# Layer norm's scaling moved from VectorE to ScalarE in a two-layer adaLN transformer kernel

## The chip, the cores and the metric

One core of a Trainium2 chip runs one launch of the kernel. The metric is the device time of a launch in microseconds. Instruction times are those of one profiled execution.

## The reference, cut to what matters

Two batches of 2048 tokens of width 128 pass through two layers. Every layer normalises its input, modulates it (a scale and a shift per feature that depend on the batch), runs attention, and does the same again ahead of a feed-forward part. Layer 0 has rotary attention and an FP4 feed-forward net, layer 1 causal attention and a mixture of experts.

```python
def _layernorm(x, axis=-1, eps=1e-05):
    m = jnp.mean(x, axis=axis, keepdims=True)
    v = jnp.var(x, axis=axis, keepdims=True)
    return (x - m) / jnp.sqrt(v + eps)

# layer 0
h = _layernorm(x) * (1 + ca) + sa
x = x + ga * _L0_attn_ref(h, Wq, Wk, Wv)        # softmax over 2048 keys, mask tril(k=1)
h = _layernorm(x) * (1 + cb) + sb
x = x + gb * _L0_ffn_ref(h, ...)                # x and h quantised to FP4 in blocks of 16
# layer 1
h = _layernorm(x) * (1 + ca) + sa
x = x + ga * _L1_attn_ref(h, qk, ov)            # causal
h = _layernorm(x) * (1 + cb) + sb
x = x + gb * _L1_ffn_ref(h, ...)                # router, 8 experts and a shared one
```

## The kernel before, in words

A batch is 16 tiles of 128 tokens, in 4 groups of 4 tiles. The program runs both batches one after the other through a loop of 32 **slots**: slot s holds layer s // 16, query tile s % 16. Every engine has its own program, written out by hand in the order of the slots, and waits for the others by semaphores. Nothing reorders the work: what stands behind a waiting instruction on its engine waits too.

In slot s, TensorE (`pe`) first transposes the normalised groups that are due (`input_turns`, `turn_group`), computes the first chunk of the next tile's scores (`scores(s + 1, 0)`, into PSUM bank 0), and then goes over the chunks of up to 512 keys: `turn_probs` transposes the probabilities of chunk c, `gate_up`, `turn_hq` and `down` are the FP4 net of an earlier tile, `scores(s + 1, c + 1)` follows, and `values` multiplies the previous chunk with V. All transposes go through one PSUM bank (`TURN`), so each waits until ScalarE has copied the one before it out. `scores(s + 2, 0)`, at the start of slot s + 1, waits until ScalarE has taken the exponential of chunk 0 of tile s + 1, since it overwrites that bank.

ScalarE (`act`) starts slot s with the exponentials of chunks 0 and 1 (`exp`), copies the transposed groups (`copy_group`), and then in each chunk copies the transposed probabilities (`copy_probs`), takes `tanh` for the FP4 net, copies `hq`, and takes the exponential of chunk c + 2. VectorE (`dve`) takes the row maxima, multiplies the rotary tables, quantises to FP4 (`quantise_h`, `fp4_input`), and ends slot s with `finish`: divide by the row sum, add to x, and take the statistics (`bn_stats`) of the finished tile. When a group's fourth tile is done, `bn_aggr` gives mean and variance (`send_statistics`), GpSimd (`pool`) raises the variance to the power -0.5 (L473), and VectorE normalises: four instructions of 128x128, `(x - mean) * rstd` (`normalise`, L1320; for the first two groups of a batch `first_normalise`, L1227).

Four norms per group are told apart. **norm0** feeds layer 0's attention (groups 2 and 3 normalised in slots 1 and 3; groups 0 and 1 of the next batch in slots 27 and 29, or in the setup). **norm1** feeds the FP4 net: normalised in slots 4, 8, 12, 16, modulated by GpSimd (`modulate_1`, L493 and L495), quantised by VectorE at the slot's end (`fp4_input`), scaled by GpSimd (`xq_scaled`), transposed by TensorE two slots later (L696 in the trace). **norm2** feeds layer 1's attention: normalised in slots 12, 16, 20, 24, transposed at the start of the next slot (L595 in the trace), copied by ScalarE twice (L1027, L1029). **norm3** feeds the router: slots 21, 25, 29, and one after the last slot.

The order on VectorE in a slot, before: `normalise_in_slot` stands behind the maxima and ahead of `quantise_h` and `finish`.

```python
for c in range(1, following):
    maximum(s + 1, c)
normalise_in_slot(s)
...
if ffn_tile(s, FFN_LAG) is not None:
    quantise_h(s - FFN_LAG)
...
finish(s)
if group_at(s, FP4_SLOT) is not None:
    fp4_input(group_at(s, FP4_SLOT))
```

## Time and profile before

| | |
|---|---|
| median of 3 runs | 736.52 us (735.71 to 736.78) |
| the profiled execution | 740.21 us, span of its instructions 738.4 us |
| TensorE busy | 647.3 us, 88% of the span |
| VectorE busy | 511.4 us, 69% |
| ScalarE busy | 319.5 us, 43% |
| GpSimd busy | 222.5 us, 30% |
| slots of batch 0, of batch 1 | from 37.9 to 329.4 us, from 329.4 to about 619 us |

Both batches go through the same program, and the trace shows the same times in the second, some 290 us later; so rows are given for batch 0. The setup comes ahead of them, and the mixture of experts behind them. A row of the timeline gives the start, the duration, the engine and the line of one or several instructions; in square brackets stands how long the engine was idle before it, and what released it. PE is TensorE, DVE VectorE, ACT ScalarE, POOL GpSimd.

### The profile page before, as it was taken

To read this page: it belongs to the slowest core of one execution; us is meant where nothing else is said; L and a number is where in the kernel's file an instruction comes from. 1 tells how busy PE (TensorE), PEld (TensorE's weight loads), DVE (VectorE), ACT (ScalarE), POOL (GpSimd) and SP (SyncE) were. 2 spreads that over 40 slices of the span, in tenths; PEclk is the share of its full clock that TensorE was granted. 3 is DMA by queue.
4 is the path that set the end of the run, shared out by engine and by line. 5 is a ranking of instruction groups with operands and counts; after the bars stand their busy time and mean duration, and the time that the engine had idled before them with its cause. 6 is when DMAs were issued, how large, how long until landed. Compare 5 with 4: busy or idle time off the path is not lost.

```text
span 738.4 us, 11039 instructions
## 1 busy us (share of the span) xinstructions
PE 647.3 (88%) x3816; PEld 504.9 (68%) x3828; DVE 511.4 (69%) x1465; ACT 319.5 (43%) x644; POOL 222.5 (30%) x225
## 2 busy tenths in 40 slices
PE   5889799988777999988889989958889998799997
PEld 4456687877556778775678777846677786576674
DVE  5957598696768667726669777596865754876665
ACT  1133344445234454543344444523445453554453
POOL 3333654343545211004455435253421102000000
PEclk9989999999879999999999999978999999999999
DMA  8400000000000000000000000000000000000001
GB/s 262 110 0 1 2 1 1 1 0 1 1 0 1 1 1 1 1 1 1 1 1 1 1 1 2 1 1 0 1 1 1 1 1 1 0 16 29 14 19 40
DMA packets 12078, 9.64 MB, mean 13 GB/s; under 512 B 1708, under 2 KB 10744, under 8 KB 12024
## 3 DMA queue, kind: packets, MB, share of 16 engines
q1 hardware_dynamic: 12024, 8.94, 4.1%
q8 instruction: 31, 0.51, 0.3%
q14 instruction: 23, 0.19, 0.1%
HBM read 6.84 MB, written 2.10 MB: 12 GB/s over the span
## 4 chain that ended last, share of the span: by engine, by line
PE 69%; DVE 18%; ACT 5%; POOL 4%; issue 4%; DMA 1%; SPq 0%; ACTq 0%; POOLq 0%
PE ps L777 14%; PE ps L647 12%; PE ps L755 8%; PE ps L606 5%; DVE xn L1320 5%; PE ps L922 4%; PE ps L924 4%; PE ps L923 4%; PE ps L800 3%; PE ps L665 2%; PE ps L801 2%; PE ps L595 2%; PE ps L816 2%; DVE row_max L1357 1%; PE ps L601 1%
## 5 line engine op out<-in xcount | busy, mean ns | idle before, releaser
L1083 ACT ACTIVATE probsT<-ps 128x512 f32<-128x512 f32 (+3 forms) x160 | 85.2, 533 | 180.4 <-PE ps L755 180.4
L777 PE MATMUL ps<-v_sb,probsT 128*128 128x129 f32 (+1 forms) x1148 | 157.1, 280 | 3.7 <-ACT probsT L1085 3.7
L777 PEld LDWEIGHTS ps<-v_sb,probsT 128*128 128x128 f32 (+1 forms) x1148 | 141.5, 191 | 10.6 <-ACT probsT L1085 5.5
L1357 DVE TENSOR_REDUCE row_max<-ps 128x1 f32<-128x512 f32 (+2 forms) x144 | 87.6, 619 | 48.3 <-PE ps L647 18.1
L755 PE MATMUL ps<-ident,probs 128*128 128x128 f32 (+1 forms) x574 | 95.7, 285 | 16.7 <-ACT probsT L1083 6.0
L755 PEld LDWEIGHTS ps<-ident,probs 128*128 128x128 f32 (+1 forms) x574 | 67.5, 143 | 49.0 <-issue 45.3
L1057 ACT ACTIVATE probs<-ps,neg_max 128x512 f32<-128x512 f32 (+7 forms) x158 | 92.8, 618 | 16.9 <-DVE neg_max L1364 16.0
L473 POOL TENSOR_TENSOR rstd<-veps,half 128x4 f32<-128x4 f32 x34 | 34.2, 1012 | 154.1 <-DVE veps L1211 153.9
L501 POOL TENSOR_TENSOR hq<-ha,hp 128x352 f32<-128x352 f32 x32 | 29.9, 934 | 139.5 <-DVE hp L1398 139.5
L647 PE MATMUL ps<-k_high,q_high 128*128 128x512 f32 (+4 forms) x112 | 46.0, 411 | 0.6 <-ACT probs L1005 0.6
L1152 ACT ACTIVATE probs<-ps 128x512 f32<-128x512 f32 x40 | 24.0, 599 | 44.7 <-PE ps L924 44.7
L1320 DVE TENSOR_SCALAR xn<-x_sb,mv,rstd 128x128 f32<-128x128 f32 x112 | 41.4, 435 | 2.2 <-POOL rstd L473 2.2
L1590 DVE TENSOR_TENSOR probs<-probs,ps 128x512 f32<-128x512 f32 x40 | 27.5, 687 | 19.9 <-ACT probs L1152 19.4
L1412 DVE SCALAR_TENSOR_TENSOR silu_g<-silu_g,ps 128x352 f32<-128x352 f32 x32 | 16.5, 516 | 34.1 <-ACT silu_g L1065 34.1
L922 PE MATMUL ps<-q_high,h_high 128*128 128x512 f32 x80 | 38.8, 485 | 0.8 <-DVE q_high L1523 0.8
L1372 DVE RECIPROCAL rsum<-ps 128x1 f32<-128x1 f32 x64 | 10.4, 163 | 40.8 <-PE ps L777 40.5
L647 PE MATMUL ps<-k_high,q_low 128*128 128x512 f32 (+4 forms) x112 | 38.7, 345 | 0.0
L647 PE MATMUL ps<-k_low,q_high 128*128 128x512 f32 (+4 forms) x112 | 38.3, 342 | 0.0
L647 PE MATMUL ps<-h_high,q_high 128*128 128x512 f32 (+2 forms) x80 | 36.9, 461 | 0.5 <-ACT probs L1057 0.5
L595 PE MATMUL ps<-ident,xn 128*128 128x128 f32 x100 | 17.6, 304 | 18.9 <-DVE xn L1320 18.0
L800 PE MATMUL ps<-w_guT,xqT 128*128 128x352 f32 x64 | 29.8, 553 | 4.6 <-ACT v_sb L998 2.5
L924 PE MATMUL ps<-q_high,h_low 128*128 128x512 f32 x80 | 32.2, 403 | 0.0
(240 smaller groups left out, 1380.8 us busy)
## 6 DMA issues: line engine op xcount, KB each, us to landing
out<-x_sb SPq DMA_DIRECT2D x8, 256.0 KB, 2.3
x_sb<-in_L_attn_x SPq DMA_DIRECT2D x2, 512.0 KB, 5.3
hT_all<-in_L_wmod SPq DMA_DIRECT2D x2, 384.0 KB
rope_cos<-table_cos SPq DMA_DIRECT2D x1, 768.0 KB, 7.5
rope_sin<-table_sin SPq DMA_DIRECT2D x1, 768.0 KB, 9.1
rope_cos<-table_cos SPq DMA_DIRECT2D x1, 256.0 KB, 4.1
rope_sin<-table_sin SPq DMA_DIRECT2D x1, 256.0 KB, 5.1
moe_raw<-in_L_ffn_expert_gate_w SPq DMA_DIRECT2D x1, 256.0 KB, 4.2
```

The source lines that it names most:

```text
L473: pool.tensor_tensor(rstd[:, kind, :], veps[:, kind, :], half[:], ALU.pow).then_inc(rstd_ready[kind], 1)
L606: pe.matmul(bank(dst), w[:], hT[:, g * BANK:(g + 1) * BANK], start=True, stop=True).then_inc(proj_ready, 1)
L647: mm = pe.matmul(ps[:, cols], q_parts[q][:, tile], keys[k][:, cols], start=(n == 0), stop=(stop and n == len(passes) - 1))
L755: mm = pe.transpose(bank(TURN, k * P, (k + 1) * P, size), probs[:, s % 2, j * P:j * P + size], ident[:])
L777: mm = pe.matmul(bank(OUT_AT, 0, V_W), probsT[0:size, n % 4, k * P:(k + 1) * P], v_sb[0:size, j, :], start=(c == 0 and k == 0), stop=(c == ...
L800: pe.matmul(bank(GATE, 0, INNER), lhs, w_guT[:, 0:INNER], start=True, stop=True)
L922: pe.matmul(dst, weights[0], high, start=start, stop=False)
L924: return pe.matmul(dst, weights[1], high, start=False, stop=stop)
L1057: act.activation(probs[:, s % 2, start:start + width], ps[:, start:start + width], ACT.Exp, bias=neg_max[:, s % 2:s % 2 + 1]).then_inc(exp ...
L1083: ins = act.activation(probsT[:, n % 4, 0:full], bank(TURN, 0, full), ACT.Copy)
L1320: ins = dve.tensor_scalar(xn[:, g, t * P:(t + 1) * P], x_tile(g * GROUP + t), mv[:, kind, t, 0:1], rstd[:, kind, t:t + 1], ALU.subtract, A ...
L1357: ins = dve.tensor_reduce(dst, ps[:, start:start + width], AX.X, ALU.max, negate=single)
```

## The change

ScalarE normalises instead of VectorE: `Identity(scale * x + bias)` with scale = rstd and bias = shift = -mean * rstd, both one number per partition. GpSimd prepares them (`scale_and_shift`, three small instructions in place of one). The four instructions of a group stand on ScalarE in chunk 1 of the slot (norm0, norm1, norm3), or behind the slot's last chunk (norm2, and the next batch's norm0). norm2's groups are transposed inside the slot, behind the first chunk, instead of at its start. Where norm1 or norm3 and norm2 end in the same slot (11, 15, 19, 23), their statistics are gathered and raised in one go (128x8 instead of twice 128x4). VectorE loses its 34 groups of four and the `tick` copies ahead of the statistics. On GpSimd `modulate_1` moves behind the rotary steps.

```diff
 def input_turns(slot):
-    firsts = (("fp4_in", FFN_LAG), ("norm2", DOWN_LAG + GROUP + 1), ("norm3", TILES + GROUP + 2))
+    firsts = (("fp4_in", FFN_LAG), ("norm3", TILES + GROUP + 2))
...
+def key_group(slot):
+    return group_at(slot, DOWN_LAG + GROUP + 1)
...
@@ gpsimd
-            def rsqrt_at(kind, n):
-                pool.wait_ge(var_ready[kind], n)
-                pool.tensor_tensor(rstd[:, kind, :], veps[:, kind, :], half[:], ALU.pow).then_inc(rstd_ready[kind], 1)
+            def scale_and_shift(kind, kinds, n):
+                rows = slice(kind, kind + kinds)
+                pool.wait_ge(var_ready[kind // 2], n)
+                pool.tensor_scalar(minus_mean[:, rows, :], mv[:, rows, :, 0], -1.0, None, ALU.mult)
+                pool.tensor_tensor(rstd[:, rows, :], veps[:, rows, :], half[:, 0:kinds, :], ALU.pow).then_inc(rstd_ready, 1)
+                powers[0] += 1
+                pool.wait_ge(rstd_ready, powers[0])
+                pool.tensor_tensor(shift[:, rows, :], minus_mean[:, rows, :], rstd[:, rows, :],
+                                   ALU.mult).then_inc(norm_ready[kind // 2], 1)
...
                 for s in range(SLOTS):
                     at = lambda first: group_at(s, first)
-                    if at(NORM1_SLOT + 1) is not None:
-                        modulate_1(at(NORM1_SLOT + 1))
                     if early_group(s, K0_SLOT + 1) is not None:
                         rope_low(early_group(s, K0_SLOT + 1), 0)
...
                         rope_sum(early_group(s, Q0_SLOT), 1)
+                    if at(NORM1_SLOT + 1) is not None:
+                        modulate_1(at(NORM1_SLOT + 1))
...
+                    if s % GROUP == GROUP - 1:
+                        scale_and_shift(0, 1 + (at(NORM2_SLOT) is not None), b * 2 * GROUPS + s // GROUP + 1)
@@ tensor
                         if c + 1 < following:
                             scores(s + 1, c + 1)
+                        if c == 0 and key_group(s) is not None:
+                            turn_group(("norm2", key_group(s)))
                         if c == min(1, n - 1) and ffn_tile(s, DOWN_LAG) is not None:
                             down(s - DOWN_LAG)
@@ scalar
+            def normalise_group(kind, batch, g):
+                for t in range(GROUP):
+                    ins = act.activation(xn[:, g, t * P:(t + 1) * P], x_sb[:, batch * TILES + g * GROUP + t, :], ACT.Identity,
+                                         scale=rstd[:, kind, t:t + 1], bias=shift[:, kind, t:t + 1])
+                return ins
...
+            first_normalise(-1, 0, 0)
             act.wait_ge(turned, 1)
             act.activation(hT[:, 0:BANK], bank(TURN), ACT.Identity, scale=mod_col[:, 0, 1:2],
                            bias=mod_col[:, 0, 0:1]).then_inc(copied, 1)
+            first_normalise(-1, 0, 1)
...
                         if c == 0 and ffn_tile(s, DOWN_LAG) is not None:
                             copy_hq(s - DOWN_LAG)
+                        if c == 0 and key_group(s) is not None:
+                            copy_group(("norm2", key_group(s)))
                         if c + 2 < n:
                             exp(s, c + 2)
+                        if c == min(1, turns - 1):
+                            normalise_in_slot(s)
+                    keys_normalised(s)
+                    if s in (NEXT_SLOT - 1, NEXT_SLOT + 1):
+                        first_normalise(b, BATCH - 1 - b, int(s > NEXT_SLOT))
+                normalise_in_slot(SLOTS + 1)
                 put_v_at(0, (b + 1) * 2 * GROUPS)
@@ vector
-                carry_wait()
-                for k in range(GROUP):
-                    ins = dve.bn_aggr(mv[:, kind, k, :], bn[:, kind, k, :])
+                for n in range(kind, kind + kinds):
+                    for k in range(GROUP):
+                        ins = dve.bn_aggr(mv[:, n, k, :], bn[:, n, k, :])
...
                     for c in range(1, following):
                         maximum(s + 1, c)
-                    normalise_in_slot(s)
-                    if s in (NEXT_SLOT - 1, NEXT_SLOT + 1):
-                        first_normalise(b, BATCH - 1 - b, int(s > NEXT_SLOT))
```

ScalarE's order from the third chunk of slot 12 into slot 13, before (`probs<-ps` is an exponential, `probsT<-ps` the copy of a transposed chunk):

```order
L1057 ACTIVATE probs<-ps,neg_max 128x129
L1083 ACTIVATE probsT<-ps 128x512 [waits pv_done,turned]
L1083 ACTIVATE probsT<-ps 128x128 [waits pv_done,turned]
L1085 ACTIVATE probsT<-ps 1x128
L1057 ACTIVATE probs<-ps,neg_max 128x512 [waits turned,max_ready]
L1057 ACTIVATE probs<-ps,neg_max 128x512
L1027 ACTIVATE h_high<-ps,mod_now 128x512 [waits turned]
L1029 ACTIVATE hT<-ps,mod_now 128x512
L1083 ACTIVATE probsT<-ps 128x512 [waits pv_done,turned]
L1065 ACTIVATE silu_g<-ps 128x352 [waits hq_grid,gu_ready]
```

The same stretch after the change:

```order
L1104 ACTIVATE probs<-ps,neg_max 128x129
L994 ACTIVATE xn<-x_sb,shift,rstd 128x128 [waits norm_ready_inner]
L994 ACTIVATE xn<-x_sb,shift,rstd 128x128 x3
L1130 ACTIVATE probsT<-ps 128x512 [waits pv_done,turned]
L1130 ACTIVATE probsT<-ps 128x128 [waits pv_done,turned]
L1132 ACTIVATE probsT<-ps 1x128
L994 ACTIVATE xn<-x_sb,shift,rstd 128x128 [waits norm_ready_inner]
L994 ACTIVATE xn<-x_sb,shift,rstd 128x128 x3
L1104 ACTIVATE probs<-ps,neg_max 128x512 [waits turned,max_ready]
L1104 ACTIVATE probs<-ps,neg_max 128x512
L1130 ACTIVATE probsT<-ps 128x512 [waits pv_done,turned]
L1112 ACTIVATE silu_g<-ps 128x352 [waits hq_grid,gu_ready]
```

The two groups of four `xn<-x_sb` are norm1 of group 2, between two copies, and norm2 of group 0, between the slot's last copy and the exponential that opens slot 13. The copies of norm2's transposed group (`h_high<-ps`, `hT<-ps`) have left their place behind the exponentials of slot 13.

TensorE's order at the start of slot 13, before (`ps<-ident,xn` transposes norm2's group, `ps<-ident,probs` a chunk of probabilities, `ps<-ident,hq` belongs to the FP4 net):

```order
L595 MATMUL ps<-ident,xn 128x128 x4
L647 MATMUL ps<-k_high,q_high 128x512
L647 MATMUL ps<-k_low,q_high 128x512
L647 MATMUL ps<-k_high,q_low 128x512
L755 MATMUL ps<-ident,probs 128x128 x4
L800 MATMUL ps<-w_guT,xqT 128x352
L801 MATMUL ps<-w_guT,xqT 128x352
L808 MATMUL ps<-ident,hq 128x128 x2
L808 MATMUL ps<-ident,hq 96x128
```

And after the change:

```order
L658 MATMUL ps<-k_low,q_high 128x512
L658 MATMUL ps<-k_high,q_low 128x512
L766 MATMUL ps<-ident,probs 128x128 x4
L811 MATMUL ps<-w_guT,xqT 128x352
L812 MATMUL ps<-w_guT,xqT 128x352
L819 MATMUL ps<-ident,hq 128x128 x2
L819 MATMUL ps<-ident,hq 96x128
L658 MATMUL ps<-k_high,q_high 128x512
L658 MATMUL ps<-k_low,q_high 128x512
L658 MATMUL ps<-k_high,q_low 128x512
L606 MATMUL ps<-ident,xn 128x128 x4
L766 MATMUL ps<-ident,probs 128x128 x4
```

The transposes of `xn` stood ahead of everything in the slot; now they stand behind the second chunk of scores and right ahead of the second chunk of probabilities, which goes through the same bank.

## Rows read from the trace of the kernel before

**Rows 1.** The page of before, parts 1 and 4: busy shares; the chain by engine

```profile
PE 647.3 (88%) x3816; PEld 504.9 (68%) x3828; DVE 511.4 (69%) x1465; ACT 319.5 (43%) x644; POOL 222.5 (30%) x225
...
PE 69%; DVE 18%; ACT 5%; POOL 4%; issue 4%; DMA 1%; SPq 0%; ACTq 0%; POOLq 0%
```

**Rows 2.** The page, part 5: groups of instructions (line, op, count | busy, mean ns | idle before)

```profile
L1320 DVE TENSOR_SCALAR xn<-x_sb,mv,rstd 128x128 f32<-128x128 f32 x112 | 41.4, 435 | 2.2 <-POOL rstd L473 2.2
...
L473 POOL TENSOR_TENSOR rstd<-veps,half 128x4 f32<-128x4 f32 x34 | 34.2, 1012 | 154.1 <-DVE veps L1211 153.9
```

**Rows 3.** Groups with shapes kept apart, ScalarE and GpSimd (same columns)

```profile
L1083 ACT ACTIVATE probsT<-ps 128x512 f32<-128x512 f32 x112 | 66.8, 597 | 115.3 <-PE ps L755 115.3
...
L1083 ACT ACTIVATE probsT<-ps 128x128 f32<-128x128 f32 x16 | 4.4, 276 | 20.8 <-PE ps L755 20.8
...
L1029 ACT ACTIVATE hT<-ps,mod_now 128x512 f32<-128x512 f32 x14 | 10.8, 772 | 7.8 <-PE ps L595 7.7
...
L450 POOL MEMSET half<- 128x4 f32 x1 | 0.1, 101 | 0.0
...
L468 POOL CAST ident_b<-ident 128x128 bf16<-128x128 f32 x1 | 0.3, 291 | 0.1
```

**Rows 4.** Timeline, slots 12 and 13 (start us, us, engine, line, [idle before <-releaser])

```profile
148.27 4.16 DVE L1320 TENSOR_SCALAR xn<-x_sb,mv,rstd 128x128 f32<-128x128 f32 x8
...
148.76 1.70 PE L777 MATMUL ps<-v_sb,probsT 128*128 128x129 f32 x12
...
149.29 1.23 ACT L1057 ACTIVATE probs<-ps,neg_max 128x512 f32<-128x512 f32 x2
...
152.49 0.73 PE L595 MATMUL ps<-ident,xn 128*128 128x128 f32 x4 [2.04 <-DVE xn L1320]
...
153.26 0.78 ACT L1027 ACTIVATE h_high<-ps,mod_now 128x512 fp32r<-128x512 f32 x1 [2.74 <-PE ps L595]
...
153.94 0.77 ACT L1029 ACTIVATE hT<-ps,mod_now 128x512 f32<-128x512 f32 x1
...
154.85 1.08 PE L755 MATMUL ps<-ident,probs 128*128 128x128 f32 x4 [0.34 <-ACT hT L1029]
```

**Rows 5.** Timeline, slots 16 to 18, VectorE and TensorE

```profile
193.98 4.16 DVE L1320 TENSOR_SCALAR xn<-x_sb,mv,rstd 128x128 f32<-128x128 f32 x8
...
198.20 1.11 PE L595 MATMUL ps<-ident,xn 128*128 128x128 f32 x4 [3.60 <-DVE xn L1320]
...
208.66 1.11 PE L696 MATMUL ps<-ident,xq 128*128 128x128 f32 x4 [2.20 <-POOL xq L518]
```

**Rows 6.** Timeline, slot 8's fp4 group as it is transposed in slot 10, TensorE

```profile
118.16 0.66 PE L696 MATMUL ps<-ident,xq 128*128 128x128 f32 x4 [1.46 <-POOL xq L518]
```

**Rows 7.** Timeline, slot 4 to 5, ScalarE and TensorE

```profile
71.93 0.66 ACT L1057 ACTIVATE probs<-ps,neg_max 128x512 f32<-128x512 f32 x1
...
73.03 0.50 PE L647 MATMUL ps<-k_high,q_high 128*128 128x512 f32 x1
```

**Rows 8.** Timeline, slot 24 to 25, ScalarE and TensorE

```profile
261.57 0.28 ACT L1083 ACTIVATE probsT<-ps 128x128 f32<-128x128 f32 x1 [0.89 <-PE ps L755]
...
263.45 0.48 PE L647 MATMUL ps<-h_high,q_high 128*128 128x512 f32 x1
...
266.73 0.63 PE L755 MATMUL ps<-ident,probs 128*128 128x128 f32 x4
```

**Rows 9.** Timeline, setup, ScalarE and TensorE

```profile
14.29 0.46 ACT L975 ACTIVATE wv_g<-ps 128x256 f32<-128x256 f32 x1
...
14.62 0.63 PE L595 MATMUL ps<-ident,xn 128*128 128x128 f32 x4 [0.80 <-ACT router_T L974]
```

**Rows 10.** Busy time by stretch: window, length, then each engine's busy us; PEclk is the granted clock

```profile
118.70:122.10 3.40, 3.40 (x12) 2.46 (x11) 2.77 (x10) 1.19 (x2) 2.08 (x3) 0.52 0.00 0
...
152.80:156.30 3.50, 3.16 (x12) 2.14 (x11) 3.26 (x13) 1.77 (x3) 1.42 (x2) 0.52 0.00 0
...
210.80:214.20 3.40, 3.40 (x11) 2.32 (x11) 1.41 (x3) 0.60 (x1) 2.94 (x3) 0.50 0.00 0
```

More of the change, by code:

```diff
@@ L204, in build @@
         unpick = sb("unpick", [P, PAIRS, P], BF16)
-        half = sb("half", [P, GROUP])
+        half = sb("half", [P, 2, GROUP])
         priority = sb("priority", [P, EXPERTS])
@@ L326, in build @@
         tanh_ready = sem("tanh_ready")
-        var_ready = [sem(f"var_ready_{k}") for k in range(3)]
-        rstd_ready = [sem(f"rstd_ready_{k}") for k in range(3)]
+        var_ready = [sem(f"var_ready_{k}") for k in ("inner", "first")]
+        rstd_ready = sem("rstd_ready")
+        norm_ready = [sem(f"norm_ready_{k}") for k in ("inner", "first")]
         xn1_ready = sem("xn1_ready")
@@ L1033, in copy_group, with normalise, normalise_in_slot, keys_normalised @@
                     act.activation(hT_group[:], bank(TURN), ACT.Identity, **args).then_inc(copied, 1)
+                def normalise(kind, n, g):
+                    act.wait_ge(norm_ready[kind // 2], b * NORM_GROUPS[kind] + n + 1)
+                    return normalise_group(kind, b, g)
+                def normalise_in_slot(s):
+                    at = lambda first: group_at(s, first + 1)
+                    if early_group(s, NORM0_SLOT + 1) is not None:
+                        normalise(2, early_group(s, NORM0_SLOT + 1), early_group(s, NORM0_SLOT + 1)).then_inc(xn0_ready, 1)
+                    if at(NORM1_SLOT) is not None:
+                        normalise(0, at(NORM1_SLOT), at(NORM1_SLOT)).then_inc(xn1_ready, 1)
+                    if at(NORM3_SLOT + 1) is not None:
+                        normalise(0, GROUPS + at(NORM3_SLOT + 1), at(NORM3_SLOT + 1)).then_inc(xn_ready, 1)
+                def keys_normalised(s):
+                    g = group_at(s, NORM2_SLOT + 1)
+                    if g is not None:
+                        normalise(1, GROUPS // 2 + g, g).then_inc(xn_ready, 1)
                 def put_v(g, n):
@@ L1221, in first_statistics @@
                 link(ins)
-                send_statistics(2, link)
-            def first_normalise(b, batch, g):
-                dve.wait_ge(rstd_ready[2], (b + 1) * GROUPS + g + 1)
-                for t in range(GROUP):
-                    ins = dve.tensor_scalar(xn[:, g, t * P:(t + 1) * P], first_tile(batch, g * GROUP + t), mv[:, 2, t, 0:1],
-                                            rstd[:, 2, t:t + 1], ALU.subtract, ALU.mult)
-                ins.then_inc(xn0_ready, 1)
+                send_statistics(2, 1, link)
             def first_rotate(b, which, link):
@@ L1346, in norm_0_statistics @@
                 def norm_0_statistics(g):
-                    statistics(2, range(g * GROUP, (g + 1) * GROUP))
+                    for t in range(g * GROUP, (g + 1) * GROUP):
+                        ins = statistics(2, t)
+                    link(ins)
+                    send_statistics(2, 1, link)
                 def maximum(s, c):
@@ L1377, in finish @@
                     dve.wait_ge(x_attn, b * SLOTS + s + 1)
-                    carry_wait()
-                    statistics(0, [i])
+                    ins = statistics(0, i)
                     if ffn_tile(s, DOWN_LAG) is not None:
-                        statistics(1, [s - DOWN_LAG])
+                        ins = statistics(1, s - DOWN_LAG)
+                    if s % GROUP == GROUP - 1:
+                        link(ins)
+                        send_statistics(0, 1 + (ffn_tile(s, DOWN_LAG) is not None), link)
                 def quantise(a, m, src, n_blocks, scales, last_wait):
```

62 lines of the change are left out of this document (19 added, 43 removed).

## The prediction

> **What bounds the kernel.** I read the shares first, then the groups, then the timeline slot by slot at each place where a norm stands. TensorE is busy 88% of the span and makes 69% of the chain that ended last; VectorE makes 18% of that chain [rows 1]. So time is to be had only where TensorE waits, and there alone a norm matters. The 112 normalising instructions of L1320 take 41.4 us [rows 2] (24 more, L1227, stand in the setup and at the batch's end); in most slots they lie beside TensorE's work. Their mean is 435 ns, but in slots 12 and 16 eight of them take 4.16 us [rows 4, 5], 520 ns each, drawn out while GpSimd works; the other 80 (both batches have those two slots) then share 41.4 - 4 x 4.16 = 24.8 us, 310 ns each, and four of the quickest take 1.1 us. In slot 12 TensorE's last products start at 148.76 and run 1.70, and then it waits 2.04 us for `xn` before it may transpose at 152.49; the first probabilities of slot 13 come at 154.85, behind ScalarE's two copies [rows 4]. In slot 16 it waits 3.60 us, and 2.20 us more in slot 18, where the FP4 group arrives through VectorE, GpSimd, VectorE and GpSimd one after the other [rows 5]. Behind such idle time the granted clock is 0.50 to 0.52 for a while, the lower of its two levels (1.2 of 2.4 GHz): TensorE is then busy without a gap and does half as much [rows 10].
>
> **The price on ScalarE.** The trace has no ScalarE instruction like the new one. The nearest is L1029: `Identity` with a scale and a bias per partition, 128x512, 772 ns. A copy costs 597 ns at 512 columns and 276 at 128, so 0.84 ns a column, and 384 columns less make 451 ns [rows 3]. The copies to `h_high` and `hT`, back to back, start 0.68 us apart [rows 4], or 0.36 at 128 columns. Four take 3 x 0.36 + 0.45 = 1.53 us; I take **1.55**, an estimate. The low end is four plain copies end to end, 1.10 us; the high end four of 451 ns end to end, 1.80. A gain is excluded: an activation isn't shorter than a plain copy of its size. The Trainium skill ("ScalarE: Activation LUTs", section on what ACT_TABLE_LOAD costs) gives 186 ns, 93 for each pointer operand, 0.833 a column and an overlap of 93 between neighbours; that would be 1.64 us for four, as an estimate, and some 2 us more over the kernel. The trace's 772 ns and 0.68 us are close to it.
>
> **The price on GpSimd.** The power of 128x4 takes 1012 ns [rows 2]. The two new instructions are as small as a memset of 101 ns and no larger than a cast of 291 [rows 3]; I take 0.15 each, with gaps 0.4 us in all per norm. The power of 128x8 lies between 1.0 (nothing per column) and 2.0 us (all per column); plain instructions of that size cost 0.1, so most of the 1.0 is the power itself, and I take 1.8.
>
> **Part by part, for one batch.** What decides is whether TensorE waits for what stands behind the norm on ScalarE: in the program that is the exponential that opens the next slot, on which the scores two tiles on wait.
> - *norm0, slots 1 and 3.* ScalarE starts as its copy ends and ends within 0.4 us of VectorE: **+0.1**.
> - *norm1, slot 4.* The exponential started at 71.93, and TensorE's scores at 73.03 [rows 7]. It now starts 1.55 later, ends near 74.1, and holds the scores up 1.1; the rotary sum that GpSimd does earlier gives most of it back in slot 5, and the FP4 group is 0.4 later: **+0.4**.
> - *norm1, slot 8.* ScalarE has a gap of 2 us there. VectorE's 1.1 goes, but its quantising then runs beside GpSimd and is drawn out, so half comes through, and TensorE's wait of 1.46 at 118.16 [rows 6] becomes 0.9: **-0.6**.
> - *slots 12 and 13.* norm2 runs at 149.3 to 150.9 on ScalarE, the exponential until 151.6, and TensorE's scores start there; the first probabilities come at 152.5 instead of 154.85 [rows 4]. The stretch at 0.52 behind it, in which TensorE is busy 3.16 us [rows 10], runs at the full clock: -1.5. Inside the slot the moved transposes cost 0.65, the two copies 1.45 that nothing hides (the next thing on TensorE needs the same bank), and the exponential behind them 0.4: +2.5. In sum **-1.3**.
> - *slots 16 to 18.* VectorE skips its 4.16. Quantising beside GpSimd costs it 2 again, and the FP4 group, transposed at 208.66 [rows 5], comes near 206.6: **-2.0**. norm2 and norm1 stand one behind the other on ScalarE, 3.1 us, but TensorE waits for the FP4 group anyway. If that cover went (the group at 204), they would be next.
> - *slots 24 and 25.* The last copy starts at 261.57, the norm runs to 263.4, the exponential to 264.1, so scores that started at 263.45 start at 264.1. The second probabilities, 266.73 before [rows 8], wait for norm2's copies until 268.2: **+1.6**. The pattern stands in slots 20 and 21 too: +1.1, and 0.8 for the power of eight, since TensorE already waited for the norm there: **+1.9**.
> - *slots 27 and 29, the next batch's norm0.* Read in the same way: the exponential is 1.2 to 1.5 later with 0.5 to spare: **+0.7** and **+1.1**. norm3, in chunk 1, lies in ScalarE's gaps: 0.
> - *the norm behind the last slot.* TensorE has nothing else to do: 0.4 for GpSimd and 0.4 more on ScalarE, less what VectorE saves: **+0.6**.
> - *ticks and joined statistics.* Some 0.07 us per slot where VectorE is late: **-0.4**.
> - *clock.* Slot 10 starts with 3.40 us at 0.52, slot 18's last stretch with 3.40 at 0.50 [rows 10]. With the wait ahead of slot 10 cut to 0.9, and slot 18's work begun 2 us earlier, I take 1.5 and 1.0 of the 1.7 that each costs: **-2.5**.
>
> The sum is 0.1 + 0.4 - 0.6 - 1.3 - 2.0 + 1.6 + 1.9 + 0.7 + 1.1 + 0.6 - 0.4 - 2.5 = -0.4, for two batches -0.8. In the setup TensorE transposed the first group at 14.62, as soon as ScalarE was through with the weights; now ScalarE normalises behind its copy of 14.29 [rows 9], so the transposes come at 16.3, and all behind follows, less 0.4 of the slow clock: +1.3. Together **+0.5**, to 740.7 us for the profiled execution of 740.21; the median of the runs shown is 3.7 lower, so 737.0. Joining the losses to the gains like this leaves an error of some 3 us.
>
> **The rivals.** *ScalarE becomes the gate and the clock gives nothing.* The new waits at slots 4, 21, 25, 28 and 30 each leave TensorE idle 1 to 1.5 us, as long as the wait of 1.46 behind which the clock fell [rows 6, 10]. The -2.5 goes, and one more stretch at half clock costs 1.7 per batch: 2 x 4.2 over the forecast, **745**; with half of it, 741. It decides from the point at which these waits and their neighbours add up to what stood ahead of slot 10. For it: in slots 20 to 29 no norm of before kept TensorE waiting for long but one, so there is little to win. The skill's rule for kernel authors (same page) sends additions and multiplications to VectorE, not ScalarE; it would come out here as this rival does, and the trace agrees so far as 1.53 us is more than 1.1.
>
> *ScalarE's norms cost 1.10 instead of 1.55.* Nine places per batch wait for them: 2 x 9 x 0.45 and 0.4 in the setup, 8.5 less: **728.5**. Against it: the 0.68 us between L1027 and L1029.
>
> *The clock gives more.* Each batch has eight stretches of 3.4 us at half clock, in slots 6, 10, 13, 17, 18 and 21. If three more of them vanish as the waits shrink, 2 x 3 x 1.7 = 10 less: **727**. For it: VectorE's long waits ahead of three of them go. Against: slots 6 and 18 still wait for the FP4 group.
>
> *The change does not do what it says*: a table load between `Exp` and `Identity`, 1.28 each time. The timeline of slot 13 has both without one, so this has no chance of its own.
>
> **How the numbers follow.** The forecast gets 0.42, with a range of its own of 734 to 741. The first rival gets 0.30, the cheap norm 0.13, the clock 0.15. Against 736.5, 0.2% is 1.5 us, about what a measurement can tell from no change. Slower: 0.17 of the forecast's share and 0.26 of the first rival's, 0.43; faster: 0.11 and 0.25 of the others', 0.36; the rest is within 0.2%, 0.21. The range of 728 to 744 leaves out the ends of the rivals.
>
> **What would show it.** Right: the norm on ScalarE at 0.45 us and four in 1.5; no wait of PE for `xn` at slots 13 and 17; a wait of PE for ScalarE's copies of about 1.5 us in slots 13, 21 and 25; scores waiting for L1104's exponentials at slots 5, 25, 28 and 30; the transposes at 208.66 some 2 us earlier from the slot 16 before it; the setup's first transposes at 16.3. Wrong: fewer than six stretches at half clock per batch, a power of 128x8 at 1.0, or VectorE late at `finish` in slots 12 and 16 as before.

## The result, and the profile after

The changed kernel takes **753.17 us** (median of 4 runs, 752.45 to 754.15) against 736.65 for the kernel before in the same comparison: ratio 1.022, interval 1.019 to 1.025. I had forecast 737.0 with a range to 744, and a chance of 0.43 for slower. The profiled execution has a span of 750.4 us, against 738.4 before.

The page of the changed kernel, part 1, and part 4's row by engine [rows 1]:

```profile
PE 646.9 (86%) x3828; PEld 504.3 (67%) x3828; DVE 462.5 (62%) x1223; ACT 370.8 (49%) x780; POOL 231.4 (31%) x269
...
PE 68%; DVE 11%; ACT 9%; POOL 6%; issue 4%; DMA 0%; SPq 0%; ACTq 0%; POOLq 0%
```

The change did what it says: VectorE lost 49 us of work and 7% of the chain, ScalarE took 51 and 4%. TensorE does the same work in 12 us more. Its waits say which work stands in its way now. The view of waits of TensorE, before (engine, tile, line, what it waited for: us in total, times, longest):

```profile
PE ps L595 <- DVE xn L1320: 18.0, 13, 3.6
PE ps L696 <- POOL xq L518: 11.0, 6, 2.3
PE ps L755 <- ACT probsT L1083: 6.0, 4, 2.2
...
PE ps L755 <- ACT hT L1029: 5.5, 8, 0.9
...
PE ps L647 <- ACT probs L1057: 0.5, 2, 0.3
```

The same view of the changed kernel (L658 are the scores, L707 the FP4 group's transposes, L766 those of the probabilities, L606 those of `xn`):

```profile
PE ps L658 <- ACT probs L1104: 20.1, 14, 3.0
PE ps L707 <- POOL xq L533: 14.6, 6, 4.6
PE ps L766 <- ACT hT L1055: 9.8, 6, 1.6
PE ps L606 <- ACT xn L994: 6.5, 7, 2.2
```

The wait for VectorE's norm (18.0) is gone, and in its place the scores wait 20.1 us for ScalarE's exponential, which they had waited 0.5 for. The copies of norm2's group cost 9.8 instead of 5.5. Groups of instructions of the changed kernel, ScalarE and GpSimd with shapes kept apart [rows 2, 3]:

```profile
L994 ACT ACTIVATE xn<-x_sb,shift,rstd 128x128 f32<-128x128 f32 x136 | 55.6, 483 | 15.6 <-POOL shift L490 15.4
...
L487 POOL TENSOR_TENSOR rstd<-veps,half 128x8 f32<-128x8 f32 x8 | 13.3, 1660 | 0.0
...
L486 POOL TENSOR_SCALAR minus_mean<-mv 128x4 f32<-128x4 f32 x18 | 4.1, 227 | 127.8 <-DVE veps L1263 127.2
```

Four of L994 take 1.65 us in a row, where I took 1.55 with bounds of 1.10 and 1.80. The power of 128x8 takes 1.66 (I took 1.8). So the prices were near right; what stood behind them was not. In slot 20 ScalarE also waits 2.25 us for GpSimd's `shift` (below).

Where the 12 us lie is seen by cutting both traces at the last step of each slot on VectorE (the reciprocals, L1372 before and L1392 after), slot by slot. A cell gives the length of the stretch in batch 0 and batch 1:

```
slots          before          after           forecast   measured
setup          46.14           47.70           +1.3       +1.6
1 to 3         18.76  18.86    18.78  18.79    +0.1        0.0  -0.1
4 to 6         28.68  28.72    28.91  28.54    +0.4       +0.2  -0.2
8               9.87   9.88     9.20   9.20    -0.6       -0.7  -0.7
10             10.12  10.11     8.76   8.76    -1.5       -1.4  -1.4
12, 13         25.75  25.75    26.40  24.78    -1.3       +0.7  -1.0
16 to 18       31.97  31.86    29.93  28.86    -3.0       -2.0  -3.0
20 to 22       24.56  24.56    28.04  28.16    +1.9       +3.5  +3.6
24, 25         12.94  12.95    16.53  16.54    +1.6       +3.6  +3.6
28 to 30       29.57  29.57    31.27  31.29    +1.8       +1.7  +1.7
```

(16 to 18 holds two terms of the forecast, -2.0 and the clock's -1.0. The end of the first batch gave +0.8 where I had +0.6; behind the last slot 125.43 became 126.83. I had taken -0.4 per batch more for the ticks and joined statistics, which no place shows.) In batch 0 half of the places came out to 0.2 us. Two are far off: slots 20 to 22 and slots 24 and 25, both in layer 1, where a slot has little work for TensorE. The timeline of the changed kernel there, ScalarE and TensorE, from slot 20's last chunk to slot 21's end:

```profile
229.82 1.65 ACT L994 ACTIVATE xn<-x_sb,shift,rstd 128x128 f32<-128x128 f32 x4 [2.25 <-POOL shift L490]
...
231.37 1.03 ACT L1104 ACTIVATE probs<-ps,neg_max 128x512 f32<-128x512 f32 x2
...
232.09 0.50 PE L658 MATMUL ps<-h_high,q_high 128*128 128x512 f32 x1 [2.99 <-ACT probs L1104]
...
237.35 0.63 PE L606 MATMUL ps<-ident,xn 128*128 128x128 f32 x4
...
238.02 0.78 ACT L1053 ACTIVATE h_high<-ps,mod_now 128x512 fp32r<-128x512 f32 x1 [0.81 <-PE ps L606]
...
238.69 0.77 ACT L1055 ACTIVATE hT<-ps,mod_now 128x512 f32<-128x512 f32 x1
...
239.61 0.41 PE L766 MATMUL ps<-ident,probs 128*128 128x128 f32 x2 [1.63 <-ACT hT L1055]
...
240.96 2.70 PE L788 MATMUL ps<-v_sb,probsT 128*128 128x129 f32 x12
```

ScalarE waits 2.25 us for GpSimd with the exponential behind it in line, normalises, and only then lets TensorE's scores go, 2.99 us late. The transposes then hold the probabilities up by 1.63. And the products with V, twelve in 2.70 us, took 1.70 for twelve elsewhere [rows 4]: the clock is down. In slots 24 and 25 of the changed kernel the same pattern stands, without the wait for GpSimd:

```profile
263.81 1.65 ACT L994 ACTIVATE xn<-x_sb,shift,rstd 128x128 f32<-128x128 f32 x4
...
266.08 0.50 PE L658 MATMUL ps<-h_high,q_high 128*128 128x512 f32 x1 [1.60 <-ACT probs L1104]
...
270.53 0.89 PE L766 MATMUL ps<-ident,probs 128*128 128x128 f32 x4 [1.63 <-ACT hT L1055]
...
272.30 2.02 PE L788 MATMUL ps<-v_sb,probsT 128*128 128x129 f32 x8
```

Busy time by stretch for the changed kernel (columns as in rows 10) has a stretch at half clock behind each of the two places:

```profile
240.10:243.50 3.40, 3.40 (x18) 3.40 (x17) 0.39 (x2) 2.91 (x7) 2.74 (x4) 0.51 0.00 0
270.80:274.20 3.40, 3.40 (x17) 3.09 (x16) 0.71 (x2) 2.13 (x5) 0.94 (x1) 0.50 0.02 5
```

Other places of the changed kernel that the prediction named (setup, slots 13 and 18):

```profile
16.32 1.11 PE L606 MATMUL ps<-ident,xn 128*128 128x128 f32 x4 [2.23 <-ACT xn L994]
...
151.34 0.50 PE L658 MATMUL ps<-k_high,q_high 128*128 128x512 f32 x1 [1.09 <-ACT probs L1104]
...
157.27 0.63 PE L766 MATMUL ps<-ident,probs 128*128 128x128 f32 x4 [1.63 <-ACT hT L1055]
...
207.10 1.12 PE L707 MATMUL ps<-ident,xq 128*128 128x128 f32 x4 [4.63 <-POOL xq L533]
```

### The profile page after: what moved, and what is told of

It reads as the page before. It is cut to its first block, busy times and chain, and to the rows that moved or that the text cites. A ratio compares the mean times of both kernels' runs of the same rounds, so it can differ in the third digit from the quotient of the medians.

```text
span 750.4 us, 10989 instructions
## 1 busy us (share of the span) xinstructions
PE 646.9 (86%) x3828; PEld 504.3 (67%) x3828; DVE 462.5 (62%) x1223; ACT 370.8 (49%) x780; POOL 231.4 (31%) x269
## 4 chain that ended last, share of the span: by engine, by line
PE 68%; DVE 11%; ACT 9%; POOL 6%; issue 4%; DMA 0%; SPq 0%; ACTq 0%; POOLq 0%
PE ps L788 14%; PE ps L658 12%; PE ps L766 8%; PE ps L617 5%; PE ps L935 4%; PE ps L937 4%; ACT xn L994 4%; PE ps L936 4%; PE ps L811 2%; PE ps L812 2%; PE ps L676 2%; PE ps L827 2%; PE ps L606 1%; PE ps L612 1%; PE ps L839 1%
## 5 line engine op out<-in xcount | busy, mean ns | idle before, releaser
L788 PE MATMUL ps<-v_sb,probsT 128*128 128x129 f32 (+1 forms) x1148 | 161.8, 286 | 3.7 <-ACT probsT L1132 3.7
L788 PEld LDWEIGHTS ps<-v_sb,probsT 128*128 128x128 f32 (+1 forms) x1148 | 146.4, 197 | 10.9 <-ACT probsT L1132 5.6
L766 PE MATMUL ps<-ident,probs 128*128 128x128 f32 (+1 forms) x574 | 93.2, 279 | 16.4 <-ACT hT L1055 9.8
L1104 ACT ACTIVATE probs<-ps,neg_max 128x512 f32<-128x512 f32 (+7 forms) x158 | 92.5, 616 | 11.5 <-DVE neg_max L1384 10.6
L766 PEld LDWEIGHTS ps<-ident,probs 128*128 128x128 f32 (+1 forms) x574 | 66.0, 140 | 46.1 <-issue 40.1
L994 ACT ACTIVATE xn<-x_sb,shift,rstd 128x128 f32<-128x128 f32 x136 | 55.6, 483 | 15.6 <-POOL shift L490 15.4
L486 POOL TENSOR_SCALAR minus_mean<-mv 128x4 f32<-128x4 f32 (+1 forms) x26 | 6.0, 230 | 166.5 <-DVE veps L1263 166.0
L1392 DVE RECIPROCAL rsum<-ps 128x1 f32<-128x1 f32 x64 | 10.5, 165 | 67.0 <-PE ps L788 66.9
L658 PE MATMUL ps<-h_high,q_high 128*128 128x512 f32 (+2 forms) x80 | 37.1, 464 | 15.8 <-ACT probs L1104 15.8
L658 PE MATMUL ps<-k_high,q_high 128*128 128x512 f32 (+4 forms) x112 | 45.0, 402 | 5.5 <-ACT probs L1104 4.4
L658 PE MATMUL ps<-k_high,q_low 128*128 128x512 f32 (+4 forms) x112 | 37.6, 335 | 0.0
L658 PE MATMUL ps<-k_low,q_high 128*128 128x512 f32 (+4 forms) x112 | 37.4, 334 | 0.0
L1434 DVE SCALAR_TENSOR_TENSOR silu_g<-silu_g,ps 128x352 f32<-128x352 f32 x32 | 16.5, 516 | 33.5 <-ACT silu_g L1112 33.5
L827 PE MATMUL ps<-w_dg,hqT 128*128 128x128 f32 (+1 forms) x192 | 29.7, 294 | 3.2 <-ACT hqT L1117 3.2
L811 PE MATMUL ps<-w_guT,xqT 128*128 128x352 f32 x64 | 27.1, 509 | 5.6 <-ACT v_sb L1024 3.5
```

Source lines behind the costliest of these rows:

```text
L658: mm = pe.matmul(ps[:, cols], q_parts[q][:, tile], keys[k][:, cols], start=(n == 0), stop=(stop and n == len(passes) - 1))
L766: mm = pe.transpose(bank(TURN, k * P, (k + 1) * P, size), probs[:, s % 2, j * P:j * P + size], ident[:])
L788: mm = pe.matmul(bank(OUT_AT, 0, V_W), probsT[0:size, n % 4, k * P:(k + 1) * P], v_sb[0:size, j, :], start=(c == 0 and k == 0), stop=(c == ...
L811: pe.matmul(bank(GATE, 0, INNER), lhs, w_guT[:, 0:INNER], start=True, stop=True)
L827: mm = pe.matmul(bank(OUT_AT, DOWN.start, DOWN.stop), hqT[0:size, k * P:(k + 1) * P], w_dg[0:size, bass.ds(b, 1), k, :].rearrange("p a n - ...
L994: ins = act.activation(xn[:, g, t * P:(t + 1) * P], x_sb[:, batch * TILES + g * GROUP + t, :], ACT.Identity, scale=rstd[:, kind, t:t + 1], ...
```

## The experiments

Theory A: what costs is ScalarE's norm2 ahead of the exponential that opens the next slot. Theory B: the mid-slot transposes with their two copies. Theory C: the half-clock stretches (TensorE at a granted clock of about 0.5) follow from its idle time ahead of them. Each kernel is compared with the kernel before on the same chip (medians of 735.1 to 737.0 us).

**norm2 back on VectorE.** In `after`, `keys_normalised(s)` leaves ScalarE, and VectorE's `normalise_in_slot` takes norm2 in its old place; the transposes stay mid-slot.

> The changed kernel (753.2 us) with one thing undone: norm2 is normalised by VectorE again, in its old place; its transposes stay mid-slot. Theory A (the loss is ScalarE's norm2 ahead of the exponential that opens the next slot: TensorE waits 1.1, 3.0 and 1.6 us for L1104 at slots 13, 21, 25, and the clock falls behind the waits of 21 and 25): those waits go, with them two half-clock stretches per batch, 2 x (5.7 + 3.4) less: 735 to 741 us. Theory B (the loss is the mid-slot transposes, whose two copies by ScalarE hold up the probabilities 1.63 us four times per batch): those waits stay, and the time stays above 746.

Measured: **735.49 us** (733.89 to 737.15), ratio to before 0.998 (0.995 to 1.000). The whole loss of 17 us is gone with this one step: slots 20 to 22 take 24.1 us instead of 28.1, 24 and 25 take 13.2 instead of 16.5, 12 and 13 take 23.6.

**Transposes back at the slot's start.** norm2 stays on ScalarE behind the last chunk:

```diff
-    firsts = (("fp4_in", FFN_LAG), ("norm3", TILES + GROUP + 2))
+    firsts = (("fp4_in", FFN_LAG), ("norm2", DOWN_LAG + GROUP + 1), ("norm3", TILES + GROUP + 2))
```

> The changed kernel with the other thing undone: norm2's groups are transposed at the start of the next slot again, the norm stays on ScalarE behind the last chunk. Theory A: the wait for ScalarE only moves from the scores to the transposes (TensorE now waits for xn ahead of everything), so 751 to 758 us, no gain worth having. Theory B: the four copies' waits of 1.63 us per batch go behind other work and most of the loss with them: 738 to 745 us.

Measured: **742.18 us** (738.52 to 742.63), ratio 1.006 (1.004 to 1.009). My expectation from theory A was wrong: two thirds of the loss go this way too. Its timeline in slot 21 says why:

```profile
229.13 1.03 ACT L1104 ACTIVATE probs<-ps,neg_max 128x512 f32<-128x512 f32 x2
...
229.28 0.66 PE L606 MATMUL ps<-ident,xn 128*128 128x128 f32 x4 [2.33 <-ACT xn L994]
...
231.63 1.09 PE L766 MATMUL ps<-ident,probs 128*128 128x128 f32 x4 [0.71 <-ACT hT L1055]
```

TensorE waits for the norm (2.33), but then transposes while ScalarE takes the exponentials, and ScalarE's two copies run while TensorE does the scores (0.71 left of them). Mid-slot, the two waits stand one behind the other, each with nothing beside it.

**Both undone.**

> Both undone at once: norm2 on VectorE and transposed at the slot's start, as before the change; norm0, norm1, norm3 and the next batch's norm0 stay on ScalarE, the statistics stay joined. Theory A: mid-slot transposition alone costs little, so within 3 us of the kernel with only norm2 back on VectorE. Theory B: 5 us or more below it. What is left against before by the slot table of the two traces: +1.6 in the setup, +1.7 per batch at slots 28 and 30, +0.8 at the batch's end, -0.7 at slot 8 and -1.4 at slot 10: about 738 to 741 us.

Measured: **735.55 us** (735.04 to 737.16), ratio 0.998 (0.996 to 1.001), the same as with norm2 alone back on VectorE. So mid-slot transposes cost nothing by themselves. TensorE's idle time in slots 12, 13, 20 to 22, 24 and 25 of batch 0 adds up so:

```
norm2 on              transposed      idle us
VectorE               slot's start      6.74
VectorE               mid-slot          7.08
ScalarE, ahead of exp slot's start      8.05
ScalarE, ahead of exp mid-slot         12.05   (the change)
ScalarE, behind exp   mid-slot          7.56   (below)
```

Each part costs most beside the other: mid-slot transposes cost 0.3 us of idle time with VectorE's norm and 4.0 with ScalarE's; ScalarE's norm costs 1.3 with the transposes at the slot's start and 5.0 with them mid-slot. In time the norm alone costs 6.6 us (742.2 against 735.6), the transposes alone nothing, both together 17.6.

**The next batch's norm0 back on VectorE** (`first_normalise` of slots 27 and 29):

> The changed kernel with only the next batch's norm0 (slots 27 and 29) back on VectorE. Theory A: the exponentials of slots 28 and 30 start on time, 0.5 and 1.4 us per batch come back (the slot table), 3.5 to 4 us in all: 749.5 us. Rival: the waits there are covered by slack later in the batch or VectorE's maxima are then late instead, 752 to 754 us.

Measured: **748.77 us** (743.97 to 750.09), ratio 1.013 (1.009 to 1.017). Slots 28 to 30 are back at 29.59 us, as before; the gain of 1.7 per batch is the term that I had forecast as 0.7 + 1.1.

This trace also bears on theory C. Slots 24 and 25 of batch 1, changed kernel first, then this one (columns as in rows 10):

```profile
553.04:569.58 16.54, 13.16 (x83) 11.13 (x82) 6.61 (x25) 10.40 (x22) 3.34 (x4) 0.90 0.00 0
...
552.70:567.70 15.00, 11.62 (x83) 9.74 (x82) 6.60 (x25) 10.12 (x22) 3.35 (x4) 1.00 0.00 1
```

TensorE has the same 83 matmuls and the same 3.38 us of idle time in both (the length less its busy time), but only the first has a stretch at half clock. So the stretch costs 1.5 us there, and the wait does not bring it every time.

**norm2 on ScalarE, but behind the exponentials.** The decisive one: nothing leaves ScalarE, four instructions change places with two.

```diff
                         exp(s, 1)
+                    if s:
+                        keys_normalised(s - 1)
                     for key in input_turns(s):
...
-                    keys_normalised(s)
                     if s in (NEXT_SLOT - 1, NEXT_SLOT + 1):
```

> The changed kernel with norm2 still on ScalarE and its transposes still mid-slot, but the four norm2 instructions stand behind the two exponentials that open the next slot instead of ahead of them. Theory A1 (what costs is that TensorE's scores wait for an exponential behind the norm): the waits for L1104 in slots 13, 21, 25 go; the norm then delays the copy of the first probabilities by up to 1.6 us, which TensorE feels only where nothing else stands between: 740 to 746 us. Rival A2 (ScalarE has no room for the norm wherever it stands in these slots): the wait moves to ScalarE's next copy, 749 to 754 us.

Measured: **735.80 us** (734.11 to 737.18), ratio 0.998 (0.995 to 1.001), better than I expected of A1. The timeline, slot 20 to 21:

```profile
226.99 1.05 ACT L1104 ACTIVATE probs<-ps,neg_max 128x512 f32<-128x512 f32 x2 [1.42 <-DVE neg_max L1385]
...
227.73 0.50 PE L658 MATMUL ps<-h_high,q_high 128*128 128x512 f32 x1 [0.62 <-ACT probs L1104]
...
227.93 1.64 ACT L994 ACTIVATE xn<-x_sb,shift,rstd 128x128 f32<-128x128 f32 x4
...
229.47 0.58 ACT L1130 ACTIVATE probsT<-ps 128x512 f32<-128x512 f32 x1
```

The scores wait 0.62 instead of 2.99 us, and the norm lies beside the scores, the transposes and the gate products. ScalarE does the same work; only its order differs. TensorE still waits for the copies six times, up to 1.6 us and 9.8 us in all, exactly as in the changed kernel; so this wait alone isn't what cost the 17 us. Slots 20 to 22 take 24.2 us instead of 28.1, with 2.3 us less idle time and one stretch at half clock less in each batch; slots 24 and 25 take 13.7 instead of 16.5.

**Waits filled with unused matmuls.** Ahead of the scores of slots 21 and 25 of the changed kernel:

```diff
+                    if s in (TILES + GROUP + 1, TILES + 2 * GROUP + 1):
+                        pe.wait_ge(gu_used, b * TILES + min(s - FFN_LAG, TILES))
+                        keep_clock(GATE, 9 if s == TILES + GROUP + 1 else 4)
                     if following:
                         scores(s + 1, 0)
```

> The changed kernel, with nine small bf16 matmuls into a free bank put on TensorE ahead of the wait for the exponential in slot 21, and four in slot 25: they compute nothing that is used and fill most of the idle 3.0 and 1.6 us. Theory C (the half-clock stretches at 240 and 270.5 come from the idle time ahead of them): these stretches go in both batches, four of 1.7 us: 746 to 748 us. Rival (the clock falls there for another reason, or falls at the next wait instead): 752 to 755 us.

Measured: **749.12 us** (744.32 to 749.85), ratio 1.016 (1.010 to 1.022). From 226 to 244 us (slots 20, 21 and the start of 22 in batch 0) TensorE now runs at the full clock:

```profile
226.00:244.00 18.00, 14.79 (x91) 11.00 (x91) 13.21 (x46) 10.77 (x26) 10.74 (x13) 1.00 0.01 1
```

Slots 20 to 22 fell from 28.0 to 25.2 us, 24 and 25 from 16.5 to 15.0, in both batches: 8.9 us in all, with the same work waiting for the same things. This supports theory C for these two places, but it is one traced execution, and the trace above lost two of these stretches without any filling. Some 6 us of it did not arrive: the setup, the end of the first batch, slots 12 and 13 and 16 to 18 of the second, and the mixture of experts were 1.0, 1.4, 1.6, 1.0 and 0.8 us longer in that execution, most of them with more time at half clock. The interval of the ratio overlaps that of the changed kernel (1.019 to 1.025), so the times alone do not tell the two apart.

**Only norm1 on ScalarE**, the rest on VectorE in the old places, transposes at the slot's start, joined statistics kept:

> The best candidate by the slot tables: of the ScalarE norms only norm1 is kept (slots 4, 8, 12, 16); norm0, norm2, norm3, the next batch's norm0, the setup and the last norm are VectorE's in their old places, norm2 is transposed at the slot's start; joined statistics and GpSimd's order as in the change. Against the kernel with norm2 undone (735.5 us): the exponentials of slots 28 and 30 are on time (3.4 us for two batches), the batch's end 1.6 us, the setup about 1: 729 to 731 us, faster than both kernels. Rival (the small savings drown in the clock's stretches, which fall elsewhere): 734 to 737 us.

Measured: **726.84 us** (724.45 to 728.13), ratio 0.987 (0.982 to 0.992), faster than both kernels and than I expected. With all norms but norm2 on ScalarE it was 735.55 us, so norm0, norm3, the next batch's norm0, the setup's and the last norm lose 8.7 us there together, of which slots 28 to 30 are 3.4. In its trace slots 20 to 22 have no stretch at half clock in either batch, with 4.1 us of idle time in them and nothing filled.

**No norm on ScalarE**, the same kernel with norm1 on VectorE too:

> The same with norm1 on VectorE too: what is left of the change is the joined statistics and powers, the missing tick copies, and GpSimd modulating behind the rotary sums. If ScalarE's norm1 makes the gains of slots 8 to 12 (0.7 + 1.4 + what slot 12 gains, per batch), this is 6 to 10 us above the kernel with only norm1 on ScalarE: 735 to 739 us. If the gains come from the joined statistics or GpSimd's order, it is within 2 us of it.

Measured: **737.60 us** (735.85 to 741.89), ratio 1.002 (0.999 to 1.005). So the joined statistics, the joined powers, the `tick` copies and GpSimd's new order are worth nothing that can be measured, and norm1 on ScalarE alone is worth 10.8 us: slot 8 takes 9.19 instead of 9.85, slots 12 and 13 take 22.9 instead of 25.8 to 26.3, some 7.7 us in both batches. Some of the rest is the clock's: slots 20 to 22, in which norm1 has no part, are 2.2 and 1.6 us shorter too, with all their stretches at half clock gone.

**norm1 and norm2 on ScalarE**, norm2 behind the exponentials and transposed mid-slot, the rest on VectorE:

> norm1 and norm2 on ScalarE, norm2 behind the exponentials that open the slot and transposed mid-slot; norm0, norm3, the next batch's, the setup's and the last norm on VectorE. By the slot tables of the two parts: slots 12 and 13 0.7 longer than with norm2 on VectorE and transposed at the slot's start, 16 to 18 0.8 shorter, 20 to 22 about even, 25 1.0 longer: within 3 us of 726.8 us, so 725 to 730. If mid-slot transposes are worth something once the exponential isn't held up, below 724.

Measured: **728.50 us** (726.04 to 733.81), ratio 0.990 (0.988 to 0.993). Behind the exponentials norm2 does no harm on ScalarE that the intervals show, but brings nothing either.

**The FP4 transposes of slot 18 behind the scores.** With only norm1 on ScalarE, TensorE still waited 5.66 us for `xq` at the start of slot 18, with work that needs no `xq` behind it. In slot 18 alone:

```diff
+                    late = s == Q1_SLOT + GROUP
                     for key in input_turns(s):
-                        turn_group(key)
+                        if not late:
+                            turn_group(key)
                     if following:
                         scores(s + 1, 0)
                     project_0_in(s)
                     project_1(s)
+                    if late:
+                        for key in input_turns(s):
+                            turn_group(key)
```

and in the same way for the copy on ScalarE.

> The kernel with only norm1 on ScalarE (726.8 us), and in slot 18 alone the transposes of the FP4 group stand behind the next tile's scores and the layer-1 projections instead of ahead of them (on ScalarE the copy moves behind those of the projections). Theory: the last wait that norm1 left, 5.66 us for GpSimd's xq in slot 18, covers about 3.5 us of that work and the half-clock stretch behind it shrinks: 2 x 3 to 2 x 4.5 less, 718 to 721 us. Rival: the copy of the FP4 group then holds up the probabilities' transposes and most comes back, 724 to 727 us.

Measured: **723.28 us** (722.40 to 724.49), ratio 0.984 (0.981 to 0.987): 3.6 less, about half of the expectation. The intervals of the two ratios overlap, but in the traces slots 16 to 18 take 27.1 us instead of 30.4 in both batches. The timeline of slot 18:

```profile
198.90 0.50 PE L659 MATMUL ps<-h_high,q_high 128*128 128x512 f32 x1 [2.92 <-ACT probs L1104]
...
202.85 0.99 PE L708 MATMUL ps<-ident,xq 128*128 128x128 f32 x4
...
204.62 0.52 PE L767 MATMUL ps<-ident,probs 128*128 128x128 f32 x3 [0.78 <-ACT xqT L1050]
```

The wait for `xq` is gone, but behind it another was hidden: the scores wait 2.92 us for an exponential, whose maximum VectorE takes only behind its quantising.

**Its waits filled.** Nine, ten and six unused matmuls at the start of slots 6, 18 and 21:

> The kernel with norm1 on ScalarE and the late FP4 transposes (723.3 us), and unused bf16 matmuls into a free bank ahead of its three longest waits in a batch: nine in slot 6 (wait of 2.74 us), ten in slot 18 (2.92), six in slot 21 (1.92). In its trace the granted clock falls to 0.50 right behind each of these waits. Theory C (the idle time ahead makes the clock fall): the stretches go without another in their place, up to 1.7 us each, 713 to 719 us. Rival (they come back at the next wait, as part of them did when two waits of the changed kernel were filled): 720 to 724 us.

Measured: **726.12 us** (725.35 to 727.10), ratio 0.985 (0.982 to 0.988), by the ratio no better than without (0.984), where I expected 4 to 10 us less. In slot 18 the filling itself waited until VectorE had freed its bank, and the scores behind it came late (slots 16 to 18 take 30.1 and 30.2 us instead of 27.1):

```profile
199.88 4.45 PE L613 MATMUL ps<-unpick,ident_b 128*128 128x512 bf16 x10 [3.30 <-DVE silu_g L1469]
```

So slot 18 was left out in the last kernel:

> The same without the filling in slot 18, where the unused matmuls themselves waited 3.3 us for VectorE to free their bank and held up the scores (that slot grew from 8.0 to 11.0 us). In slots 6 and 21 the filling took the half-clock stretch away (11.77 to 11.24 us, and 8.84 to 7.44). Theory C: 0.5 and 1.4 to 1.9 us per batch below the kernel without filling (723.3 us): 719 to 721 us. Rival (stretches come back at slot 18, at the batch's end or in the mixture of experts): 722 to 725 us.

Measured: **719.46 us** (717.18 to 720.67), ratio **0.975** (0.971 to 0.979), 17.5 us below the kernel before and the fastest of all. That is 0.9 points below the kernel without filling, with intervals apart; some of it may be the clock falling elsewhere. Slot 21's work runs at the full clock in both batches:

```profile
224.00:227.40 3.40, 2.47 (x15) 1.59 (x13) 2.95 (x10) 2.00 (x4) 1.86 (x2) 1.00 0.00 0
504.00:507.40 3.40, 2.47 (x15) 1.90 (x14) 2.62 (x10) 2.00 (x5) 2.25 (x3) 1.00 0.01 2
```

## Why the prediction was wrong

*Right.* The prices on ScalarE and GpSimd (1.65 us against 1.55, 1.66 against 1.8); the small ones of GpSimd were a little low (200 to 240 ns where I took 150). The terms of slots 1 to 10 and 28 to 30 in batch 0 and the batch's end came out to 0.3 us each; the transposes of the setup at 16.32, where I had 16.3. VectorE's wait for the norm gone from slots 13 and 17, the stretches at half clock gone from slot 10 and, in one batch, from 13. The FP4 group of slot 18 was transposed 17.7 us behind the end of slot 15 instead of 19.7, so the 2.0 of that term came. "ScalarE becomes the gate" had the right mechanism: the scores wait for L1104 at slots 5, 13, 17, 21, 25 and 30. At slot 28, where I expected it too, they do not, and the one at 17 (2.33 us) I had left to the cover of the FP4 group.

*Right by luck.* The setup took +1.6 where I had +1.3. The same setup took 46.9 to 49.0 us in the traces of the first six kernels above, so this agreement is one execution's.

*The clock's term (-2.5 per batch, and the -1.5 in slot 13): this is the step that failed.* I took away stretches at half clock for waits that shrink, and added none for those that grow; only the first rival added one. In slot 10 the gain came (-1.4 in both batches). In slot 13 it came in one batch. In slots 16 to 18 the time lost to the clock (half the length of the stretches) fell from 6.8 to 3.4 us in both batches, but in batch 0 these slots got only the 2.0 us shorter that the FP4 group explains: the time won lay ahead of TensorE's wait for that group, which grew to 4.63 us. In batch 1 half of the time at half clock behind that wait went as well, and they got 3.0 shorter. And in slots 20 to 22 (forecast +1.9, measured +3.5) and 24 and 25 (+1.6, measured +3.6) TensorE's idle time grew by 1.8 and 1.9, as forecast, and on top each place got one stretch more, 1.7 us each, behind the new waits. That is 3.4 of the 3.6 us by which these two places missed, and 6.8 for two batches. Added up over slots 10 to 25, the clock was to give 8.0 us and cost 1.3: 9 of the 11.5 us between the +0.5 forecast for the profiled execution and the 12.0 measured. The count of stretches alone does not show this. Between slots 4 and 25, with 3.4 us counted as one, batch 1 of the changed kernel has five of them and batch 0 seven, against eight and eight before, so even my sign of being wrong, "fewer than six", came up, and what decides is where they fall. Filling the waits took the stretches of slots 20 to 25 away again, and with them the one that slot 21 had before; why the clock falls behind some of these waits and not behind others stays open.

*Slots 12 and 13 (forecast -1.3, measured +0.7 and -1.0).* What isn't the clock's was right within half a microsecond. The stretch at half clock that I had taken away came back in batch 0, behind the copies' wait at 157.27.

*The rival's price.* I gave rival one 745 us, by taking the clock's gain away and adding one stretch of 1.7. Of the 5.0 us of gain it took away, 3.8 stayed; the added stretches were two per batch. The rest is slots 12 and 13, the mixture of experts, and the step from the profiled execution to the median, which follows.

*From the profiled execution to the median.* The two spans differ by 12.0 us, the medians by 16.5. I subtracted 3.7 us from the sum, since the profiled execution of before lay that much above the median. But the profiled execution was long at a granted clock of 0.948, while the executions of before within 1 us of its medians stand at 0.955 to 0.964, around the changed kernel's 0.958 to 0.960. So some of the half-clock time that I took away as a gain of the change was not there in the median execution, and was counted twice. This fault is worth up to 3.7 us of the 16 by which I missed; which stretches the median execution lacks no trace shows.

*The rule of the Trainium skill.* "ScalarE: Activation LUTs" of the Trainium skill (its rule for kernel authors) sends plain additions and multiplications to VectorE, and I had made its outcome a rival. The runs agree with it for the next batch's norm0, and for norm2 ahead of the exponentials. For norm2 behind them, and for norm0 in slots 1 and 3 (18.8 us either way), they show no difference. For norm1 they differ: ScalarE has room behind the second chunk, and the kernel takes 10.8 us less with it there. The 520 ns that I read for VectorE in slots 12 and 16 were an average that hides what happens. VectorE's eight instructions in slot 12 of the kernel before, and GpSimd's modulation beside them:

```profile
L1320 DVE TENSOR_SCALAR xn<-x_sb,mv,rstd x8: 334/340/1411, 148.3 to 152.1; 128x128 f32<-128x128 f32 x8
...
149.46 1.30 POOL L493 TENSOR_TENSOR xn<-xn,mod_row_now 128x512 f32<-128x512 f32 x1 [4.32 <-DVE xn L1320]
...
150.84 1.26 POOL L495 TENSOR_TENSOR xn<-xn,mod_row_now 128x512 f32<-128x512 f32 x1
```

(334/340/1411 are the shortest, the median and the longest in ns.) Six of the eight take 0.34 us; one takes 1.29 and ends 0.1 us behind the first of GpSimd's two, one takes 1.41 and ends 0.1 us behind the second. Two of norm2's instructions stood still, each for one of GpSimd's on norm1, and with norm1's four gone to ScalarE slots 12 and 13 are 2.9 us or more shorter.

## What to carry to other kernels

On an engine with in-order work, ask of each instruction that is moved to it what stands behind it and who waits for that: here, with the transposes mid-slot, the same four instructions cost 17 us ahead of two exponentials and nothing behind them. A move that is free alone can be dear beside another that takes away its cover: the mid-slot transposes cost nothing beside VectorE's norm (735.5 and 735.6 us) and 11 beside ScalarE's (753.2 against 742.2). So price them as a pair, place by place. And a wait on TensorE that grows can cost the clock behind it as much as itself (1.7 us behind waits of 1.6 and 3.0 here): whoever takes half-clock stretches away in the sum where waits shrink must add them where waits grow, and one that lies ahead of a wait for another engine may cost nothing, as in slots 16 to 18 of batch 0.

## What the runs showed of the hardware

The kernel before isn't one number. Over the executions beside these experiments it took from 730.7 us at a granted clock of 0.969 to 741.5 at 0.950, with the same program on the same chip, so it varies by about 10 us with the time at half clock; the changed kernel was always at 0.958 to 0.960. With matmuls whose result nobody uses put into a wait, the stretch behind it was gone in slots 6, 21 and 25, in both batches of each trace; in slot 18, where they had to wait for their own bank, they cost 3 us. What makes the clock fall at one wait and not at another of the same length stays open: in slot 10 the kernel without a norm on ScalarE had the stretch in one batch and not in the other, with the same work, and slots 20 to 22 had none with only norm1 on ScalarE, but one and two with the late FP4 transposes added, with about 4 us of idle time each time.
